# Two-layer mixture of experts on one core: TensorE's shared expert groups written as loops, and three waits of GpSimd for its own scatters

## The reference, cut to what matters

```python
# layer 0: 16 experts of width 256, each token goes to one
feat = x @ W[subject] + b[subject]
logits = feat @ w_router.T;  e = top1(logits);  score = sigmoid(logits[e])
shared = silu(feat @ w_gate.T) * (feat @ w_up.T) @ w_down.T
x = x + shared + expert_e(score * feat)
# layer 1: 8 experts of width 512, each token goes to two, capacity 1280 tokens per expert
h = relu(x @ W1[lang] + b1[lang]);  feat = layernorm(x + h @ W2[lang] + b2[lang]) * gamma + beta
first, second choice = top2(softmax(feat @ router_w)), positions in each expert by a running count
shared = silu(feat @ sw1 + sb1) @ sw2 + sb2
x = x + 0.1 * shared + g1 * expert_first(feat) + g2 * expert_second(feat)
```

## Time and profile before

| what | value |
|---|---|
| median of 3 runs | 533.72 us (531.76 to 535.09) |
| the profiled execution's own time | 532.79 us |
| its span, first to last instruction | 531.0 us |
| busy: TensorE, VectorE, ScalarE, GpSimd | 447.7, 240.2, 247.4, 256.3 us |
| granted TensorE clock, mean | 0.939 of full |

### The profile page before, as it was taken

How to read it: one execution, slowest core, us unless ns; L and a number is a source line. 1 busy time by engine, 2 the same in 40 slices (tenths; PEclk the granted TensorE clock), 3 DMA queues, 4 the chain that set the end, 5 groups by cost and what they waited for, 6 DMA issues and landing times.

```text
span 531.0 us, 9984 instructions
## 1 busy us (share of the span) xinstructions
PE 447.7 (84%) x3129; PEld 384.3 (72%) x3130; DVE 240.2 (45%) x708; ACT 247.4 (47%) x593; POOL 256.3 (48%) x272
## 2 busy tenths in 40 slices
PE   6798879965999998899997879918999999999900
PEld 4698746644777775477786869908999999999800
DVE  1344486422555554244868865212333233323237
ACT  2234486202555553356456534403555555555424
POOL 3003567771555555500246777760555555655510
PEclk8989999996999999899999799977999999999965
DMA  9999921111322220800001111113234324331169
GB/s 255 398 308 356 393 63 45 55 50 46 78 71 68 78 64 8 237 10 2 11 30 42 45 51 46 55 40 100 66 116 123 107 68 141 109 79 34 35 175 307
DMA packets 66131, 57.96 MB, mean 109 GB/s; under 512 B 9485, under 2 KB 53152, under 8 KB 66099
## 3 DMA queue, kind: packets, MB, share of 16 engines
q1 hardware_dynamic: 58402, 43.99, 27.7%
q0 software_dynamic: 7168, 12.51, 7.3%
q10 hardware_dynamic: 528, 1.05, 0.5%
HBM read 30.28 MB, written 29.47 MB: 113 GB/s over the span
## 4 chain that ended last, share of the span: by engine, by line
PE 63%; POOL 12%; issue 12%; DVE 5%; DMA 5%; ACT 1%; POOLq 1%; SPq 0%; DVEq 0%; ACTq 0%
PE PS L1459 13%; PE PS L1145 8%; POOL rows L568 7%; PE PS L1189 6%; PE PS L1381 4%; POOL rows L536 4%; PE PS L1268 4%; PE PS L1447 4%; PE PS L1448 4%; PE PS L1449 4%; PE PS L1253 2%; PE PS L1255 2%; PE PS L1254 2%; PE PS L1368 2%; PE PS L1206 2%
## 5 line engine op out<-in xcount | busy, mean ns | idle before, releaser
L586 POOL DMA_INDIRECT back<-grp_y,grp_i x80 | 79.6, 996 | 71.9 <-DVE grp_y L1102 58.0
L568 POOL DMA_INDIRECT rows<-disp,slot x64 | 64.9, 1014 | 66.8 <-DVE slot L946 47.2
L1459 PE MATMUL PS<-w2r,act 128*128 128x128 f32 x640 | 77.7, 275 | 0.0
L1459 PEld LDWEIGHTS PS<-w2r,act 128*128 128x128 f32 x640 | 74.7, 191 | 0.0
L735 ACT ACTIVATE act<-PS,b1r 128x256 f32<-128x256 f32 x160 | 62.8, 475 | 14.5 <-PE PS L1449 14.5
L547 POOL DMA_INDIRECT back<-act,blk_i x48 | 47.0, 980 | 42.0 <-DVE act L906 21.3
L1102 DVE TENSOR_TENSOR grp_y<-PS,b2r 128x256 f32<-128x256 f32 x40 | 17.0, 425 | 89.3 <-PE PS L1459 84.4
L596 ACT ACTIVATE xh<-PS 128x256 fp32r<-128x256 f32 (+1 forms) x48 | 20.0, 418 | 74.2 <-PE PS L1145 74.2
L1447 PE MATMUL PS<-xh,w1h 128*128 128x256 f32 x160 | 48.3, 302 | 0.0
L526 POOL TENSOR_TENSOR w_gul<-w_raw,w_guh 128x512 fp32r<-128x512 f32 x16 | 21.0, 1336 | 50.1 <-ACT w_guh L596 50.1
L1448 PE MATMUL PS<-xl,w1h 128*128 128x256 f32 x160 | 44.9, 281 | 0.0
(11 more groups left out here) (216 smaller groups left out, 946.0 us busy)
## 6 DMA issues: line engine op xcount, KB each, us to landing
rows<-zrow SPq DMA_DIRECT2D x32, 258.0 KB, 5.4
grp_x<-rows SPq DMA_DIRECT2D x40, 129.0 KB, 2.3
w_raw<-in_f_gate_up SPq DMA_DIRECT2D x8, 512.0 KB, 7.7
back<-zrow SPq DMA_DIRECT2D x8, 512.0 KB, 6.9
back<-back SPq DMA_DIRECT2D x16, 256.0 KB, 4.6
blk_x<-rows SPq DMA_DIRECT2D x48, 64.5 KB, 1.8
acc<-in_x SPq DMA_DIRECT2D x8, 256.0 KB, 5.2
y0g<-back SPq DMA_DIRECT2D x8, 256.0 KB, 3.2
```

Of the source, the lines that this page charges most:

```text
L568: gp.indirect_dma_start(rows1, bass.IndirectOffsetOnAxis(ap=slot[:, k, t:t + 1], axis=0), disp[:, t, :], None, bounds_check=E1 * CAP - 1, ...
L586: gp.indirect_dma_start(back1, bass.IndirectOffsetOnAxis(ap=grp_i[v % NX][:, u:u + 1], axis=0), grp_y[k][:, u, :], None, bounds_check=last ...
L1459: last = mm(PS[5 + k][:, u * P:(u + 1) * P], act[k][:, c, u * P:(u + 1) * P], w2r[e][:, c, :], start=c == 0, stop=c == C1 - 1)
```

## The change

Three waits are added on GpSimd. In layer 0, before tile 16, it waits until the 16 scatters before have landed. In layer 1, before the first tile of the second choices, it waits until the second half of the first choices has landed, and before tile 16 of the second choices until their first half has.

On TensorE the middle groups of both shared experts become loops of three iterations with two groups in each. Group numbers are then register values: the semaphore values waited for are computed from them, and so is the place in `featT` in layer 0. The buffers (`act`, `xh`, `xl`) keep fixed names by the parity of the group. The order of the groups stays. In layer 1 up(2) is no longer cut in two: the counting products of the second choices now stand ahead of the whole of up(2).

```diff
                 if t % (NT // 2) == 0:
                     pool.wait_ge(slots0, t // (NT // 2) + 1)
+                if t == NT // 2:
+                    pool.wait_ge(sc0, 16 * t)
                 if t % G == 0:
                     pool.wait_ge(scaled, t + G)
...
                     if k == 1 and t == 0:
                         pool.wait_ge(slots1, NT // RT + 1)
+                        pool.wait_ge(sc1[0][1], 16 * HT)
+                    if k == 1 and t == HT:
+                        pool.wait_ge(sc1[1][0], 16 * HT)
...
             def shared0_up(n):
+                feat = featT[:, ds(n * GP, GP)]
                 for c in range(C0):
                     for w, b in ((shg, 2 * c), (shu, 2 * c + 1)):
-                        if n >= 1:
-                            pe.wait_ge(act_done, C0 * (n - 1) + c + 1)
-                        mm(PS[b][:, :], w[:, c * P:(c + 1) * P], featT[:, n * GP:(n + 1) * GP],
-                           start=True, stop=True).then_inc(pe_gu, 1)
+                        if not (isinstance(n, int) and n == 0):
+                            pe.wait_ge(act_done, n * C0 - C0 + (c + 1))
+                        mm(PS[b][:, :], w[:, c * P:(c + 1) * P], feat, start=True, stop=True).then_inc(pe_gu, 1)
...
-            for n in range(1, NG):
-                shared0_up(n)
-                shared0_down(n - 1)
-            shared0_down(NG - 1)
+            shared0_up(1)
+            shared0_down(0, 0)
+            with pe.Fori(0, NG // 2 - 1) as it:
+                for u in range(2):
+                    shared0_up(it * 2 + (2 + u))
+                    shared0_down(it * 2 + (1 + u), (1 + u) % 2)
+            shared0_down(NG - 1, (NG - 1) % 2)
...
             rank1(NT // RT - 1)
-            shared1_down(0)
-            shared1_up(1)
-            shared1_up(2, range(C1 // 2))
+            shared1_down(0, 0)
+            shared1_up(1, 1)
             pe.wait_ge(b_tk, NG)
             pe.wait_ge(mk1, NT // RT + 1)
...
-            shared1_up(2, range(C1 // 2, C1))
-            shared1_down(1)
-            for n in range(3, NG):
-                shared1_up(n)
-                shared1_down(n - 1)
+            with pe.Fori(0, NG // 2 - 1) as it:
+                for u in range(2):
+                    shared1_up(it * 2 + (2 + u), u)
+                    shared1_down(it * 2 + (1 + u), 1 - u)
```

More of the change, by code:

```diff
@@ L1214, in shared0_up, with shared0_down @@
             def shared0_up(n):
+                feat = featT[:, ds(n * GP, GP)]
                 for c in range(C0):
                     for w, b in ((shg, 2 * c), (shu, 2 * c + 1)):
-                        if n >= 1:
-                            pe.wait_ge(act_done, C0 * (n - 1) + c + 1)
-                        mm(PS[b][:, :], w[:, c * P:(c + 1) * P], featT[:, n * GP:(n + 1) * GP],
-                           start=True, stop=True).then_inc(pe_gu, 1)
-            def shared0_down(n):
-                pe.wait_ge(act_done, C0 * (n + 1))
-                if n >= 1:
+                        if not (isinstance(n, int) and n == 0):
+                            pe.wait_ge(act_done, n * C0 - C0 + (c + 1))
+                        mm(PS[b][:, :], w[:, c * P:(c + 1) * P], feat, start=True, stop=True).then_inc(pe_gu, 1)
+            def shared0_down(n, k):
+                pe.wait_ge(act_done, n * C0 + C0)
+                if not (isinstance(n, int) and n == 0):
                     pe.wait_ge(acc0, n)
@@ L1227, in shared0_down @@
                     for c in range(C0):
-                        last = mm(tile(PS[4], i), tile(act[n % 2][:, c, :], i), shd[:, c, :],
+                        last = mm(tile(PS[4], i), tile(act[k][:, c, :], i), shd[:, c, :],
                                   start=c == 0, stop=c == C0 - 1)
@@ L1334, in rank1, with shared1_up @@
                 last.then_inc(pe_rank1, 1)
-            def shared1_up(n, chunks=range(C1)):
+            def shared1_up(n, k):
                 pe.wait_ge(s_sp, n + 1)
-                for c in chunks:
-                    if n >= 1:
-                        pe.wait_ge(s_sl, C1 * (n - 1) + c + 1)
+                for c in range(C1):
+                    if not (isinstance(n, int) and n == 0):
+                        pe.wait_ge(s_sl, n * C1 - C1 + (c + 1))
                     high, low = sw1h[:, c * P:(c + 1) * P], sw1l[:, c * P:(c + 1) * P]
-                    mm(PS[c][:, :], high, xh[n % 2][:, :], start=True, stop=False)
-                    mm(PS[c][:, :], high, xl[n % 2][:, :], start=False, stop=False)
-                    mm(PS[c][:, :], low, xh[n % 2][:, :], start=False, stop=True).then_inc(s_gu, 1)
+                    mm(PS[c][:, :], high, xh[k][:, :], start=True, stop=False)
+                    mm(PS[c][:, :], high, xl[k][:, :], start=False, stop=False)
+                    mm(PS[c][:, :], low, xh[k][:, :], start=False, stop=True).then_inc(s_gu, 1)
             keep_busy(PS[1], 7)
@@ L1353, in _ @@
                     pe.wait_ge(b_var, NG)
-                    shared1_up(0)
+                    shared1_up(0, 0)
                 if n + 1 < NG:
@@ L1408, in _, with shared1_down @@
                     last.then_inc(b_bt, 1)
-            def shared1_down(n):
-                pe.wait_ge(s_sl, C1 * (n + 1))
-                if n >= 1:
+            def shared1_down(n, k):
+                pe.wait_ge(s_sl, n * C1 + C1)
+                if not (isinstance(n, int) and n == 0):
                     pe.wait_ge(s_ac, n)
@@ L1416, in shared1_down @@
                     for c in range(C1):
-                        last = mm(tile(PS[4], i), tile(act[n % 2][:, c, :], i), sw2[:, c, :],
+                        last = mm(tile(PS[4], i), tile(act[k][:, c, :], i), sw2[:, c, :],
                                   start=c == 0, stop=c == C1 - 1)
@@ L1479, in _ @@
             q_tr(0, 0)
-            shared1_down(NG - 1)
+            shared1_down(NG - 1, (NG - 1) % 2)
             q_stage(0, *q_args(0), first=True)
```

## The result

The changed kernel takes 538.39 us (median of 11 runs), the kernel before 534.31 us (11 runs). The ratio is 1.0101, 95% interval 1.0070 to 1.0132, so 5.4 us slower with 3.7 to 7.1 us as bounds; the two medians by themselves are 4.1 us apart. The forecast was 539.5 us, in a range of 535.5 to 543.5, and a cost of 6.2 us. Single runs of either kernel scatter over some 8 us, so the parts are read from traces and the sums from ratios.

The account below looks back on a forecast made before the run. GpSimd's scatter queue was taken to bound both stretches before the experts, with TensorE under cover. Three waits sum to 6.2 us, added to 532.79 us (539.0) or from the median (539.9): forecast 539.5 us, range 535.5 to 543.5.

Parts of the forecast that it names:

- What bounds the two stretches: Before the experts in both layers, GpSimd's scatter queue sets the end; TensorE has 8.9 and 13.0 us of cover.
- The price of a wait, landing + 0.80 - 1.28 us: At GpSimd's three new waits: landing plus restart less one issue period; 2.1, 1.9 and 2.2 us, sum 6.2.
- The restart's 0.80 us: On GpSimd, the next scatter starts 0.80 us after what it waited for, as read at earlier waits.
- The second scatter behind a wait: On GpSimd, it may start 1.67 instead of 1.28 us after the first: up to 0.4 us more per wait.
- The loops at nothing: TensorE's shared-expert loops: three iterations cost 0 to 3.3 us per layer, under TensorE's cover, so priced at nothing.
- The counting products at nothing: Layer 1, TensorE: issued earlier but started when VectorE is ready, after about 2.3 us of waiting; price 0.
- The clock at the restarts: TensorE after idling in both layers: same slow start expected; full clock at once would give about 1.8 us per layer.
- Cheap waits: Rival at GpSimd's three waits: short landings and restart nearer 0.30 us, cost 3.7 to 5.2 us, 536.5 to 538.5; chance 0.25.
- The clock that pays back: Rival at TensorE's restarts: full clock at once, -1.8 us per layer against 3.7 us of waits, 532.9 us; chance 0.12.
- Loops out of their cover: Rival in layer 0: iterations over 3.6 us make TensorE the bound; at 5 us each, 543.5 us; chance 0.03.
- Waits that do nothing: Rival at GpSimd's three waits: what they ask for has always landed; held impossible, no chance given.

Follow-up runs that it names:

- seven waits: The kernel before with the three waits and four more, before tiles 8 and 24 in layer 0 and of the second choices: 547.08 us, ratio 1.0233.
- waits with two scatters in hand: The changed kernel with each of its three waits two scatters later, asking for the same landings: 533.54 us, ratio 0.9972.
- down(7) first: The kernel before with layer 1's last shared down product ahead of the expert stage's first transposes: 531.81 us, ratio 0.9935.
- the first try of the gains: The kernel before with down(7) ahead of the first transposes, 9 products of zeros before layer 0's blocks and 10 behind down(7): 528.17 us, ratio 0.9836.
- TensorE kept busy: The changed kernel with products of zeros on TensorE, 9 before layer 0's blocks and 18 before layer 1's experts: 536.44 us, ratio 1.0051.
- the gains with six: The kernel before with down(7) ahead of the first transposes, 9 products of zeros before layer 0's blocks and 6 behind down(7): 527.64 us, ratio 0.9853.

## Why the prediction was right, point by point

**What bounds the two stretches.** GpSimd's queue, with TensorE under it. Right: the waits alone move the time by the whole 1.06%, the loops alone by 0.00%.

**The price of a wait, landing + 0.80 - 1.28 us.** The form is right, shown from two sides: seven waits cost about in proportion, and waits with two scatters in hand cost nothing. The terms against the trace after:

| wait | predicted | trace after |
|---|---|---|
| layer 0 | 2.1 | 2.15 |
| behind the first choices | 1.9 | 2.91 |
| middle of the second choices | 2.2 | 1.92 |
| sum | 6.2 | 7.0 |

The middle one was mis-sized. I took the landing of 2.4 us that the same scatter had before; it is 3.3 us now, within the bound of 3.9. The wait does not make it late: without a wait there it landed after 3.1, 3.2 and 3.0 us in the traces of the loops alone, of down(7) first and of the first try of the gains. In the kernel before it was the scatter just ahead of it, at 310.51 us, that took the 3.9 us. So the ordinary landing of this one scatter in one trace was the wrong row to go by, and half of the way to the longest would have been nearer. The third went the other way: the late landing of 3.1 us was not this scatter's habit, and taking it half into account overpaid by 0.3 us. The restart's 0.80 us is right to 0.05. The second scatter behind a wait, for which I kept 0.4 us each in the range, comes 0.1 us late at the middle wait and not at all at the two others. The same three waits come to 7.0 us here, 6.5 with the waits alone and 5.8 with TensorE kept busy, where the middle landing was an ordinary one. By the ratio the whole is 5.4 us with 3.7 to 7.1, which holds both the forecast and the trace's sum. That 6.2 lies so near to all of them is partly luck: an error of 1.0 us one way and one of 0.3 us the other stand in it.

**The loops at nothing.** Right. The cover was 8.9 and 13.0 us and the loops used at most 0.6 of it. The seam of 1.11 us, from the block loop, was the wrong row: that loop loads eight blocks' offsets into registers at its seam, the new loops do register arithmetic only, and behave as the expert loop does. That the loads make the 1.11 us is argued from the programs; no run takes them away alone. The Trainium skill ("Runtime: NRT & Kernel Launch", section on instruction fetch mechanics) says that a taken branch to a page that is not held stalls the engine for a fetch. By the estimate of 0.94 us for one that would have been 2.8 us in each layer; TensorE's timeline shows no such stall in either new loop.

**The counting products at nothing.** Right in effect. TensorE waited 1.36 us for VectorE and not 2.3. The products started 16.31 us behind the first scatter of the third part of the first choices, where it had been 15.69 us, so the slots came 0.7 us later too, with 3 us to spare. That is not the move's doing: with the waits alone, where the counting products stand in their old place, it is 16.35 us. One slip changes nothing: the landing that the wait of L575 asks for comes eight scatters before it is needed, not ten.

**The clock at the restarts.** The slow starts stayed, as expected: a granted clock of 0.60 and 0.50 in the five microseconds from 125 and 366 us. They are worth 1.1 us in layer 0 and 2.2 in layer 1 (3.57 against 5.81 us), where I had 1.8 and 1.8.

**The rivals.** Cheap waits: the time does not exclude them, for 538.39 us lies in their 536.5 to 538.5. (That range mixes two bases; 3.7 to 5.2 us on the profiled execution's 532.79 is 536.5 to 538.0.) The traces do: the restart is 0.85 us and not 0.30, and the three waits come to 7.0, 6.5 and 5.8 us in three traces, all above 5.2. The estimate worked out from the Trainium skill ("DMA: Bandwidth & Descriptors", section on the anatomy of one DMA), 2.15 us to completion, gave 5.0 us for the three; the landings at the three places were 2.6, 3.3 and 2.4 us, so the measured rows decide, though the ratio's interval would allow 5.0 too. The clock that pays back: its price is there, 2.7 us when TensorE is kept busy (0.1 to 5.2), but nothing in the change brings it about. Loops out of their cover: excluded. Waits that do nothing: excluded.

## What to carry to other kernels

A wait of GpSimd for its own last scatter cost the landing plus the restart less one issue period here, about 2 us. Before paying that, ask for the same landings a few transfers later: with two in hand it was free here, with 0.7 us to spare at an ordinary landing. And read such a landing from several scatters around the place, not from the one row that stands there. An engine that is idle for 9 or 13 us is not only cover; look at what it has to do first afterwards, for that work may fit into the idle time (3.5 us here), and the clock of its restart can be worth keeping up (2.7 us).

## What the runs showed of the hardware

- GpSimd's restart from a wait on a DMA landing is 0.85 us (316.26 to 317.11), near that from a wait on VectorE, 0.80 us. Behind the wait after the first choices the second scatter starts 0.42 us after the end of the first instead of 0.30, in all four traces that have this wait; behind the others it starts after 0.30 or 0.31.
- The landing of the scatter in front of the wait behind the first choices was 3.3 us in the changed kernel, 3.2 us with the waits alone and 3.2 us with seven, and 2.4 us in the kernel before; in the run with TensorE kept busy it was 2.3 us, an ordinary one. Without a wait there it was 3.1, 3.2 and 3.0 us in three traces, and in two more (the kernel before, 3.9 us, and the gains with six, 3.4 us) the scatter ahead of it was the late one. So the wait is not the cause; what is, stays open.
- Loops on TensorE with register values in their waits and in an operand's place ran without a gap at the seam (steps of 6.3 to 6.4 and 5.22 us), while the block loop, which also loads registers there, idles 1.11 us.
